# Edge stage of a graph network layer: ScalarE's weighted slots in a buffer of their own, summed by one VectorE reduction

## What is computed

```
e  = einsum('ehd,ehd->eh', k[src], q[dst]) / sqrt(256)   # 103,125 edges, 4 heads of 64
ex = exp(e - emax[dst])                                  # maximum per target node and head
ft2[dst] = sum of ex * v[src] / sum of ex                # per target node, head by head
```

## Time and profile before

| | |
|---|---|
| median of 3 runs | 2310.03 us (2309.44 to 2310.37) |
| the profiled execution's own time | 2306.91 us |
| its span, first to last instruction | 2305.0 us |
| busy share of the span | PE 79%, DVE 78%, ACT 65%, POOL 57% |
| edge stage, first gather to last `part` | 104.9 to 1461 us |

### The profile page before, as it was taken

The page is one execution under the profiler, slowest core; times in us unless marked ns, Lnnn a source line. Parts: engine busy times, 40 slices in busy tenths (PEclk is TensorE's granted clock), DMA queues, the critical chain, the costliest instruction groups (busy, mean ns, idle before and its releaser), DMA issues. The chain is left out here.

```text
span 2305.0 us, 43942 instructions
## 1 busy us (share of the span) xinstructions
PE 1829.8 (79%) x12285; PEld 1288.0 (56%) x12285; DVE 1798.8 (78%) x3579; ACT 1505.6 (65%) x5102; POOL 1304.2 (57%) x1281
## 2 busy tenths in 40 slices
PE   7768787788776688887888871387999769999996
PEld 3423333333333566666666650233888669999995
DVE  7389999999998999999999998555899864444442
ACT  2267787777776587787877874587555355555553
POOL 0177777777777777777777777276000014444442
PEclk9878898999988688897978975599999889999998
DMA  8677777777777777777777777475010282222223
GB/s 231 189 229 226 225 229 230 226 222 228 219 225 225 211 226 224 231 226 231 228 230 235 222 234 220 123 201 161 12 32 29 69 294 42 37 36 36 36 37 77
DMA packets 213270, 394.32 MB, mean 171 GB/s; under 512 B 46354, under 2 KB 140637, under 8 KB 213005
## 3 DMA queue, kind: packets, MB, share of 16 engines
q0 software_dynamic: 91392, 278.99, 43.0%
q1 hardware_dynamic: 96848, 90.41, 13.3%
q10 hardware_dynamic: 24829, 22.64, 3.0%
HBM read 346.47 MB, written 48.65 MB: 171 GB/s over the span
## 5 line engine op out<-in xcount | busy, mean ns | idle before, releaser
L802 POOL DMA_INDIRECT ring<-kv_tab,idx x1008 | 1029.3, 1021 | 412.4 <-issue 294.6
L1120 ACT ACTIVATE val<-ring,val 128x64 f32<-128x64 f32 x2016 | 530.1, 337 | 55.6 <-DVE part L901 51.9
L853 DVE TENSOR_TENSOR prod<-ring,tile_bank 128x1024 f32<-128x1024 f32 x252 | 302.1, 1215 | 32.8 <-DMA ring<-kv_tab,idx 32.2
L860 DVE TENSOR_REDUCE score<-prod 128x16 f32<-128x1024 f32 x252 | 299.1, 1211 | 0.0
L2137 POOL DMA_INDIRECT x_sum<-e_yw,to_row x56 | 123.7, 2210 | 219.3 <-DVE e_yw L2163 197.9
L2122 POOL DMA_INDIRECT xr<-rows,from_row x56 | 57.3, 1024 | 286.7 <-issue 286.4
L2212 PE MATMUL e_h<-e_xT,e_now 128*128 128x128 f32 x1792 | 210.9, 277 | 0.8 <-DVE e_now L2153 0.8
L2212 PEld LDWEIGHTS e_h<-e_xT,e_now 128*128 128x128 f32 x1792 | 206.1, 193 | 1.2 <-DVE e_now L2153 1.2
L2227 PE MATMUL e_yps<-e_now,e_hT 128*128 128x256 f32 x896 | 202.5, 379 | 0.0
L890 DVE TENSOR_TENSOR val<-val 128x1040 f32<-128x1040 f32 x126 | 155.9, 1237 | 52.6 <-ACT val L1120 52.4
L2177 ACT ACTIVATE e_now<-e_w_all 128x2048 f32 x56 | 106.9, 1912 | 131.2 <-PE e_yps L2227 131.2
(11 more groups left out here) (423 smaller groups left out, 4719.1 us busy)
## 6 DMA issues: line engine op xcount, KB each, us to landing
loaded<-parts SPq DMA_DIRECT2D x150, 130.0 KB, 2.3
e_w_all<-L_ffn_W SPq DMA_DIRECT2D x16, 1024.0 KB, 12.2
parts<-part ACTq DMA_DIRECT2D x126, 130.0 KB
q_win<-q_tab SPq DMA_DIRECT2D x126, 128.0 KB
ring<-kv_tab,idx POOLq DMA_INDIRECT x1008
kv_tab<-kv_t SPq DMA_DIRECT2D x25, 224.0 KB
xn_buf<-x SPq DMA_DIRECT2D x25, 125.0 KB
x_sum<-x_buf SPq DMA_DIRECT2D x25, 125.0 KB
```

Source lines behind the costliest of these rows:

```text
L802: pool.indirect_dma_start(out=ring[:, n % RING, e, :], out_offset=None, in_=t.kv_tab, in_offset=bass.IndirectOffsetOnAxis(ap=idx[n % 6][:, ...
L853: dve.tensor_tensor(prod[half][:, :, :], ring[:, n % RING, at, 0:F], bcast(q_ps[n % 2].unsqueeze(1), 128, L // 2, F), ALU.mult).then_inc(q ...
L860: dve.tensor_reduce(score[:, at, :], prod[half][:, :, :].rearrange("p s (h d) -> p s h d", h=HG), AX.X, ALU.add).then_inc(reduced, 1)
L1120: one = act.activation(val[n % 2][:, e, h, 0:DG], ring[:, n % RING, e, F + h * DG:F + (h + 1) * DG], ACT.Copy, scale=val[n % 2][:, e, h, D ...
```

## The change

`val` keeps slots 0 to 3 alone. ACT's four slots go to a new buffer `act_val` [128, 4, 65, 4] in which the slot is the innermost index: each of ACT's 16 activations a tile writes 64 elements that stand 16 bytes apart, and takes its scale from there. The exponentials of the eight slots, one activation before (L1113), are two of 16 elements each. The first fold now adds only DVE's slots 2 and 3 onto 0 and 1 (520 elements) and no longer waits for ACT; `fold_on` adds the remaining two (260). A new `sum_act` waits for ACT's slots and adds up four neighbours into `act_sum` in one TENSOR_REDUCE (260 sums out of 1040 elements). `fold_last` adds `act_sum`. `fold` stands ahead of `mix(n, 2, 2)` and `mix(n, 3, 0)`, `sum_act` right behind `fold_on`. The number of buffers, the ring, the gathers and PE's work stay.

```diff
-        val = [s.sb(f"val{i}", [128, L, HG, DG + 1]) for i in range(2)]
+        val = [s.sb(f"val{i}", [128, L // 2, HG, DG + 1]) for i in range(2)]
+        act_val = [s.sb(f"act_val{i}", [128, HG, DG + 1, L // 2]) for i in range(2)]
+        act_sum = s.sb("act_sum", [128, HG * (DG + 1)])
...
             def fold(n):
                 dve.wait_ge(val_ready, n + 1)
-                dve.wait_ge(act_val_ready, n + 1)
-                dve.tensor_tensor(v[:, 0:4, :], v[:, 0:4, :], v[:, 4:8, :], ALU.add).then_inc(folding, 1)
+                dve.wait_ge(exp_ready, n + 1)
+                dve.tensor_tensor(v[:, 0:2, :], v[:, 0:2, :], v[:, 2:4, :], ALU.add).then_inc(folding, 1)
...
-                dve.tensor_tensor(v[:, 0:2, :], v[:, 0:2, :], v[:, 2:4, :], ALU.add).then_inc(folding, 1)
+                dve.tensor_tensor(v[:, 0, :], v[:, 0, :], v[:, 1, :], ALU.add).then_inc(folding, 1)
+
+            def sum_act(n):
+                dve.wait_ge(act_val_ready, n + 1)
+                wait(dve, folded, n)
+                dve.tensor_reduce(act_sum[:, :], act_val[n % 2][:, :, :, :].rearrange("p h d s -> p (h d) s"), AX.X, ALU.add
+                                  ).then_inc(sum_ready, 1)
...
+                dve.wait_ge(sum_ready, n + 1)
-                dve.tensor_tensor(part[n % 3][:, :], v[:, 0, :], v[:, 1, :], ALU.add).then_inc(folded, 1)
+                dve.tensor_tensor(part[n % 3][:, :], v[:, 0, :], act_sum[:, :], ALU.add).then_inc(folded, 1)
...
                 if now:
                     less_top(n)
+                if old:
+                    fold(n - 1)
                 mix(n, 2, 2)
                 mix(n, 3, 0)
-                if old:
-                    fold(n - 1)
                 if n + AHEAD + 1 < TILES:
                     compare(n + AHEAD + 1)
                 if old:
                     fold_on(n - 1)
+                    sum_act(n - 1)
...
-                act.activation(val[n % 2][:, :, :, DG], less[n % 2][:, :, :], ACT.Exp, scale=1.0 / float(F) ** 0.5).then_inc(exp_ready, 1)
+                act.activation(val[n % 2][:, :, :, DG], less[n % 2][:, 0:L // 2, :], ACT.Exp, scale=1.0 / float(F) ** 0.5)
+                act.activation(act_val[n % 2][:, :, DG, :], less[n % 2][:, L // 2:, :].rearrange("p s h -> p h s"), ACT.Exp,
+                               scale=1.0 / float(F) ** 0.5).then_inc(exp_ready, 1)
...
-                    one = act.activation(val[n % 2][:, e, h, 0:DG], ring[:, n % RING, e, F + h * DG:F + (h + 1) * DG], ACT.Copy,
-                                         scale=val[n % 2][:, e, h, DG:DG + 1])
+                    one = act.activation(act_val[n % 2][:, h, 0:DG, e - L // 2], ring[:, n % RING, e, F + h * DG:F + (h + 1) * DG], ACT.Copy,
+                                         scale=act_val[n % 2][:, h, DG, e - L // 2:e - L // 2 + 1])
```

More of the change, by code:

```diff
@@ L881, in weigh @@
                 dve.wait_ge(w_ready, n + 1)
-                dve.tensor_tensor(val[n % 2][:, 0:L // 2, :, 0:DG],
+                dve.tensor_tensor(val[n % 2][:, :, :, 0:DG],
                                   ring[:, n % RING, 0:L // 2, F:2 * F].rearrange("p s (h d) -> p s h d", h=HG),
```

## The result

The changed kernel takes 2291.97 us (median of 4, 2290.72 to 2293.82) against 2309.74 us (median of 4, 2305.88 to 2310.37): ratio 0.9916, 95% interval 0.9902 to 0.9931, some 18 us faster. The forecast was 2303, with a range of 2290 to 2325. The profiled execution has a span of 2291.0 us, 14.0 less than before; the edge stage in it, first gather to last `part`, takes 1335.3 us (107.3 to 1442.6), 21.1 less than before (104.9 to 1461.3).

The account below looks back on a forecast made before the run. The prediction took DVE and POOL, coupled by a ring of four tiles, as two nearly full lines bounding the edge stage. Its terms, +42.4 - 24.6 - 24.8 = -7.0 us, led to 2303 us, range 2290 to 2325.

Parts of the forecast that it names:

- What bounds the kernel: Edge stage: DVE and POOL are two nearly full lines; DVE instructions with two SBUF inputs lengthen gathers, 76 us in all.
- Without a break: POOL's 1008 gathers in the edge stage were said to run from 104.9 to 1443.2 us with no pause.
- Parts 1 and 2: DVE's changed folds and new reduction of 1.23 us: +0.34 us a tile, +42.4 us over 126 tiles (to +47.7).
- rival E: DVE's reduction pays for each sum, 0.27 us for 260 runs of four: +34 us, 2337 us; chance 8%.
- Part 3: DVE's wait for ACT, moved to `sum_act`: 24.6 of 52.4 us goes, with ACT given 0.76 us more a tile.
- rival D: ACT's strided writes cost more, losing from 0.056 us each; at 0.08 us 2325; sign: activations over 0.39; chance 15%.
- rival B: Writes 16 bytes apart cost ACT nothing: waits change by -34.5 instead of -24.6, sum -17, 2293 us; chance 18%.
- Part 4: POOL's gathers: lengthening falls from 76 to 30 to 45 us, and DVE's waits for gathers shrink by 24.8 us.
- Part 5: `fold` ahead of mix steps delays `dve_floor` and `dve_scale` by 0.6 us, covered by ACT's idle time: counted as nothing.
- The sum: Whole change: +42.4 - 24.6 - 24.8 = -7.0 us, with DVE setting the end of the edge stage.
- Rivals C: Gathers do not get shorter: POOL's 1340 us stay and DVE's gain turns into waits at L853; 2310 us; chance 17%.

Follow-up runs that it names:

- two-inputs kernel: Changed kernel with `sum_act`'s reduction replaced by an addition of `act_val` to itself, two SBUF inputs, into an unread buffer: 2324.8 us, 1.0064 to the kernel before.
- the additions: Kernel before the change, but DVE folds its own four slots to one, then waits for ACT and folds ACT's by two additions: 2282.71 us, ratio 0.9873.

## Why the prediction was right, and where it was off

The forecast was 11 us too high, and the result lies 2 us inside the lower end of its range; only 47% stood on any gain over 0.2%. What follows is about the parts.

**What bounds the kernel.** Right, and it carried the rest: two full lines, DVE and POOL, with POOL's gathers held by DVE instructions of two SBUF inputs. The two-inputs kernel showed it with an instruction of another kind in the same place and of the same duration, and `times_q` that the number of elements written is not the cause. "Without a break" was not quite so: 3.6 us of waits for the ring were there. The rule of the Trainium skill (SBUF — State Buffer, Who interferes with whom), that a DVE instruction with two SBUF inputs contends with a GpSimd instruction that reads SBUF and a reduction does not, agrees: 27 us held with the reduction, 90 with the addition. What that section infers beside it, that a tensor_tensor leaves descriptor generation alone, does not save the gathers here; which part of a gather is held the traces do not tell.

**Parts 1 and 2, +42.4 us.** Measured: 348.0 - 296.8 = 51.2, less 0.08 x 126 = 10.1 for one more overlap, and 4.9 because `fold_last` now stands idle 7.5 instead of 2.6 us behind the reduction: +46.0. The reduction took 1.226 for the forecast 1.23; runs of four cost nothing, rival E is refuted.

**Part 3, -24.6 us.** This is the term that was mis-sized: the forecast gave ACT work that ACT did not get. The wait fell from 52.4 to 14.1 us; 6.3 came back at L855, a wait that I had not named: -32.0. I had given ACT 0.76 us a tile more to do, 0.61 of it for writes 16 bytes apart, by L1113's and L872's durations. An activation did become longer, and by more than my upper bound, 0.061 us against 0.046. At 0.398 us it is over the 0.39 that the prediction had named as the sign of rival D, a slower kernel:

```profile
L1132 ACT ACTIVATE act_val<-ring,act_val 128x64 f32<-128x64 f32 x2016 | 559.2, 398 | 51.0 <-DVE part L910 46.6 <-issue 2.0
```

But ACT did not get slower. Two pieces of ACT's timeline, the changed kernel's and then that of the additions, which writes neighbours:

```profile
602.22 1.11 ACT L1132 ACTIVATE act_val<-ring,act_val 128x64 f32<-128x64 f32 x4
603.18 0.57 ACT L1164 ACTIVATE phi<-bank_f 125x496 f32<-125x496 f32 x1
```

```profile
1075.79 1.05 ACT L1129 ACTIVATE val<-ring,val 128x64 f32<-128x64 f32 x4
1076.74 0.57 ACT L1168 ACTIVATE phi<-bank_f 124x500 f32<-124x500 f32 x1
```

In both the next activation starts 0.95 to 0.96 us after the first of the four, and so it is everywhere: the median is 0.955 in the changed kernel (342 such groups) and in the kernel before (328). The 0.06 us lie at an activation's end, where the next one covers them; four take 0.06 more together, not each. Likewise the second exponential starts 0.10 us behind the first. So ACT got at most some 0.10 us a tile, not 0.76, each wait shrank by up to 1.40, and in the nine tiles of the earlier trace rows that makes 1.40 + 0.86 + 0.50 + 0.52 + 1.40 = 4.68 of 6.96, 67%, -35: rival B, which had 18%. I priced a step in an engine's line by an instruction's duration where its pitch counts. For DVE I had taken the overlap off; for ACT I had not looked for it. Of the 16-byte lines (Advanced Engine Details and Errata, SBUF Cachelines, in the Trainium skill) the trace shows a penalty in the duration of ACT's activations and, at 1040 bytes, in the reduction's rate; a rule that speaks of a penalty says nothing yet of who pays it.

**Part 4, -24.8 us.** Right, a little short: -28.5. The gathers' lengthening fell to 27 us where 30 to 45 were forecast, and POOL waits for ring slots. That part of the gain is not independent of part 3: with the wait back in place nothing is left of it, and with the gathers held again the later wait leaves the kernel 0.6% slower than before.

**Part 5, nothing.** Agrees: DVE waits nowhere for ACT's steps of the other block more than before, apart from L855.

**The sum.** +46.0 - 32.0 - 28.5 = -14.5. All of these terms lie in the edge stage, which became 21.1 us shorter: in it DVE was busy 1251.5 us before and 1287.1 after (+35.6) and idle 104.9 and 48.2 (-56.7). The stages outside took 7.1 us longer in the profiled execution after, so the spans differ by only 14.0; that the terms add up to about the same is chance. Of the 6.6 us that they leave over, 5.5 are busy time: the folds explain 51.2 - 10.1 = +41.1, while instructions that the change does not touch came out shorter (L853 302.1 us, L855 299.4). Why they did, and why the other stages took longer, the two profiles do not say. The medians differ by 17.8. Rivals C, D and E are refuted; B's mechanism is what happened.

## What to carry to other kernels

An engine at 57% busy was a full line: look for gaps that are all alike and durations with a long tail, and ask what runs on the other engines in just those. Sum what a slow partner delivers last, and do your own part first: in the kernel with additions, a wait behind DVE's own folds was worth 1.3% although DVE did 0.26 us a tile more, and it needed neither the new buffer nor the new layout. Price a step on a pipelined engine by the distance between starts, in the line of the engine that it lengthens.

## What the runs showed of the hardware

- A gather by POOL (128 rows) takes 0.946 us and 0.30 us of issue. If a DVE instruction with two SBUF inputs runs 0.13 us after its start, it ends as a rule 0.82 to 0.83 us after that instruction, later when another such one follows at once. A TENSOR_REDUCE does not hold it (97 gathers, mean 947 ns), nor does a tensor_tensor that reads one of its inputs from PSUM (220, mean 946).
- ACT's activation of 64 elements takes 337 ns when it writes neighbours and 398 at 16 bytes' distance, with the same 0.24 us between starts. DVE's reduction of 1040 elements takes 1226 ns when it reads neighbours and 1945 at 1040 bytes' distance.
- The same program took 2310 us on some chips and 2827 to 2867 on others, where PE's results came up to 14.7 us behind the recorded end of the matmul, against 0.02 us on the faster ones.
